# Moving the tail of each batch in a two-layer transformer kernel: transposes, router and feed-forward issued some tenths of a step later

## The reference

```python
qkv = x @ qkv_w + qkv_b                       # 16 heads of 16, a window of 128 keys
local = softmax(mask(q k^T / 4)) @ v
remote = latent_attention(x) @ rout_w + rout_b # 64 pooled tokens per sequence, 4 heads
gate = sigmoid(local @ gl_w + remote @ gr_w)   # one number per row and head
x = layernorm(x + (gate*local + (1-gate)*remote) @ out_w + out_b)

z = (x - mean(x)) * rsqrt(var(x) + eps) * ln_g + ln_b
probs = softmax(batchnorm(mean_over_rows(z)) @ Wr + br); e = argmax(probs)
h = relu(z @ W_down[e] + b_down[e])            # one expert for the whole sequence
x = layernorm(x + (h @ W_up[e] + b_up[e]) * probs[e])
```

## The kernel before

| job | engine, line | what it does |
|---|---|---|
| `gate`, `mix` | DVE, L1450 to L1457 | mixed rows A from local and remote part |
| `turn_a`, `a_in` | PE L1178, ACT L1299 | A transposed, copied to SBUF (two halves) |
| `r`, `r_in` | PE L1102, DVE L1402 | remote part of batch b+1 |
| `out`, `add` | PE L1186, DVE L1461 | output projection, residual sum (two halves) |
| `stats` | DVE, L1345, L1348, L1467, L1468 | means and variances |
| `root` | POOL, L1559 | 1/sqrt of the variances |
| `u_r` | POOL, L1544 | remote part of batch b+1 times a gate weight, 128x1024 |
| `nb` | DVE, L1472, twice | minus mean times 1/sqrt |
| `new` | ACT, L1303 (4) and L1306 (4) | normalised rows z, then the residual x |
| `turned` | ACT, L1270 and three DMA issues L1273 | row maxima of batch b+1 into the stacks |
| `turn_z`, `z_in` | PE L1193, ACT L1311 | z transposed, scaled, column sums |
| `zb`, `rl`, `rl_in` | DVE L1478 to L1480, PE L1199, DVE L1484 | router logits |
| `r_exp`, `choose`, `near` | ACT L1315, DVE L1490, ACT L1321 | expert chosen, its weights copied |
| `h`, `h_in` | PE L1205, ACT L1328 | down projection |
| `up`, `fin` | PE L1214, DVE L1498 | up projection, residual sum (two halves) |
| `stats2`, `root2`, `nb2`, `new2` | DVE L1345 to L1505, POOL L1563, DVE L1508, ACT L1332 | last layer norm |
| `store` | SP, L1018 | x to HBM |

## Time and profile before

### The profile page before, as it was taken

How to read it: one execution, slowest core, us unless ns; L and a number is a source line. 1 busy time by engine, 2 the same in 40 slices (tenths; PEclk the granted TensorE clock), 3 DMA queues, 4 the chain that set the end, 5 groups by cost and what they waited for, 6 DMA issues and landing times. The chain is left out here.

```text
span 1852.8 us, 25416 instructions
## 1 busy us (share of the span) xinstructions
PE 1390.9 (75%) x9117; PEld 880.4 (48%) x9117; DVE 971.0 (52%) x2245; ACT 633.7 (34%) x1201; POOL 292.6 (16%) x278
## 2 busy tenths in 40 slices
PE   4386878887787868714998558988888888888853
PEld 1143445443444445413997325555555555454532
DVE  4254555454545445331776345657474757565622
ACT  0023243333333334302553113344434444434332
POOL 2010001010101000033111311313131313111110
PEclk9678999898999989956999579989898989898966
DMA  3643526353535060085221446426161616060000
GB/s 111 95 80 58 83 56 87 86 74 91 77 87 86 30 89 2 1 267 154 73 70 41 85 77 95 75 41 103 24 103 26 103 31 101 26 89 1 13 12 12
DMA packets 70924, 130.45 MB, mean 70 GB/s; under 512 B 7936, under 2 KB 60816, under 8 KB 67344
## 3 DMA queue, kind: packets, MB, share of 16 engines
q1 hardware_dynamic: 66192, 119.63, 34.2%
q0 software_dynamic: 3072, 8.41, 1.7%
q10 hardware_dynamic: 1536, 0.79, 0.2%
HBM read 84.19 MB, written 43.81 MB: 69 GB/s over the span
## 5 line engine op out<-in xcount | busy, mean ns | idle before, releaser
L467 DVE TENSOR_REDUCE first_maxima<-bank 128x1 f32<-128x512 f32 (+3 forms) x352 | 220.7, 638 | 324.8 <-PE bank L299 323.8
L421 ACT ACTIVATE arena<-pair 128x512 f32<-128x512 f32 x320 | 184.4, 600 | 419.4 <-PE pair L324 418.1
L1416 DVE TENSOR_REDUCE second_maxima<-bank 128x2 f32<-128x512 f32 (+1 forms) x224 | 152.6, 685 | 240.8 <-PE bank L1125 233.2
L1284 ACT ACTIVATE second_probs<-pair 128x512 f32<-128x512 f32 (+1 forms) x256 | 138.2, 543 | 321.0 <-PE pair L1149 279.0
L298 PE MATMUL bank<-first_k_stack,first_q_stack 96*128 96x256 bf16 (+3 forms) x512 | 143.8, 315 | 82.8 <-DMA first_k_stack<-parked 57.6
L323 PE MATMUL pair<-first_q_stack,first_k_stack 99*128 99x512 bf16 (+3 forms) x512 | 138.6, 310 | 10.6 <-DMA first_q_stack<-first_m_turned 8.8
L278 PE MATMUL bank<-first_xT,w_qkv 128*128 128x512 f32 x256 | 133.5, 650 | 11.2 <-DVE first_halves L452 5.6
L1146 PE MATMUL pair<-second_q_stack,second_k_stack 99*128 99x256 bf16 (+1 forms) x512 | 101.2, 283 | 16.8 <-ACT second_probs L1284 13.5
L298 PEld LDWEIGHTS bank<-first_k_stack,first_q_stack 96*128 96x128 bf16 x512 | 51.1, 101 | 124.8 <-DMA first_k_stack<-parked 60.8
L1123 PE MATMUL bank<-second_k_stack,second_q_stack 96*128 96x256 bf16 (+1 forms) x512 | 94.8, 280 | 20.5 <-DMA second_k_stack<-parked 18.7
L342 PE MATMUL pair<-arena,first_values 128*32 128x512 f32 (+3 forms) x1024 | 105.1, 530 | 1.4 <-ACT arena L421 1.4
(11 more groups left out here) (311 smaller groups left out, 2575.7 us busy)
## 6 DMA issues: line engine op xcount, KB each, us to landing
parked<-first_parts SPq DMA_DIRECT2D x32, 384.0 KB, 2.8
first_q_stack<-parked SPq DMA_DIRECT2D x48, 256.0 KB, 8.5
first_k_stack<-parked SPq DMA_DIRECT2D x48, 256.0 KB, 18.9
parked<-second_parts SPq DMA_DIRECT2D x32, 384.0 KB, 2.5
second_q_stack<-parked SPq DMA_DIRECT2D x48, 256.0 KB, 9.0
second_k_stack<-parked SPq DMA_DIRECT2D x48, 256.0 KB, 18.6
sorted_x<-first_zero SPq DMA_DIRECT2D x3, 1670.5 KB, 13.4
expert_xs<-sorted_x SPq DMA_DIRECT2D x39, 128.5 KB, 2.2
```

The source lines that it names most:

```text
L421: act.activation(PT[:, s:s + len(heads), lo:lo + each], ex[n % 3][:, 0:len(heads) * each].rearrange("p (h q) -> p h q", h=len(heads)), ACT ...
L467: dve.tensor_reduce(nm[:, i, qt, heads[0]:heads[0] + len(heads)], mx[n % 2][:, 0:wide].rearrange("p (h k) -> p h k", h=len(heads)), AX.X, ...
L1284: act.activation(PT[:, s:s + len(heads), lo:lo + each], ex[n % 2][:, 0:len(heads) * each].rearrange("p (h q) -> p h q", h=len(heads)), ACT ...
L1416: dve.tensor_reduce(nm[:, i, qt, heads[0]:heads[0] + len(heads)], mx[n % 2][:, :].rearrange("p (h k) -> p h k", h=len(heads)), AX.X, ALU.m ...
```

## The change

Twenty-four kinds of jobs of the tail get other numbers. `turn_a` moves by 0.1 of a step, `out` by 0.08, the first statistics by 0.05 (their later parts by less or a little back), `turn_z` by 0.18, the router's jobs by 0.15 to 0.08, `h` by 0.12, `up` by 0.06 and the last statistics by 0.03. No instruction is added or removed.

```diff
--- before.py
+++ after.py
@@ -900,25 +900,25 @@
         at(t + 1.22, "gate", b)
         at(t + 1.3, "mix", b)
         for c in range(KC):
-            at(t + 1.45 + 0.1 * c, "turn_a", b, c)
-            at(t + 1.55 + 0.1 * c, "a_in", b, c)
-            at(t + 1.76 + 0.1 * c, "out", b, c)
-            at(t + 1.84 + 0.1 * c, "add", b, c)
-            at(t + 2.4 + 0.1 * c, "turn_z", b, c)
-            at(t + 2.48 + 0.1 * c, "z_in", b, c)
-            at(t + 3.42 + 0.1 * c, "up", b, c)
-            at(t + 3.5 + 0.1 * c, "fin", b, c)
+            at(t + 1.55 + 0.1 * c, "turn_a", b, c)
+            at(t + 1.63 + 0.1 * c, "a_in", b, c)
+            at(t + 1.84 + 0.1 * c, "out", b, c)
+            at(t + 1.9 + 0.1 * c, "add", b, c)
+            at(t + 2.58 + 0.1 * c, "turn_z", b, c)
+            at(t + 2.65 + 0.1 * c, "z_in", b, c)
+            at(t + 3.48 + 0.1 * c, "up", b, c)
+            at(t + 3.55 + 0.1 * c, "fin", b, c)
         for n, kind in enumerate(("stats", "root", "nb", "new")):
-            at(t + 2.0 + 0.1 * n, kind, b)
-            at(t + 3.65 + 0.08 * n, kind + "2", b)
-        at(t + 2.7, "zb", b)
-        at(t + 2.8, "rl", b)
-        at(t + 2.88, "rl_in", b)
-        at(t + 2.94, "r_exp", b)
-        at(t + 3.0, "choose", b)
-        at(t + 3.1, "near", b)
-        at(t + 3.2, "h", b)
-        at(t + 3.3, "h_in", b)
+            at(t + 2.05 + 0.08 * n, kind, b)
+            at(t + 3.68 + 0.08 * n, kind + "2", b)
+        at(t + 2.85, "zb", b)
+        at(t + 2.95, "rl", b)
+        at(t + 3.0, "rl_in", b)
+        at(t + 3.05, "r_exp", b)
+        at(t + 3.1, "choose", b)
+        at(t + 3.18, "near", b)
+        at(t + 3.32, "h", b)
+        at(t + 3.38, "h_in", b)
         at(t + 3.97, "store", b)
     return [item[2:] for item in sorted(out)]
```

## The result

| | before | after |
|---|---|---|
| median, us | 1853.03 (20 runs) | 1865.82 (20 runs) |
| lowest to highest, us | 1843.8 to 1861.07 | 1853.1 to 1875.84 |
| the profiled execution, us | 1854.6 | 1854.04 |
| its six periods, `turn_a` of batch 0 to `turn_a` of batch 6, us | 534.04 | 556.78 |

The change made the kernel slower: ratio 1.0081, 95% interval 1.006 to 1.0103, some 13 to 15 us. The median lies at the upper edge of the range given; the direction was forecast wrong.

A forecast was written before the change was run, and what follows sets the result against it. PE was taken to bound layer 1, as ACT and DVE mostly wait for it. The terms, -7.0 - 8.4 + 2.8 + 8.4 = -4.2 us, gave 1850.4 us for the profiled execution, 1849 us median; range 1834 to 1866 us.

The forecast's parts named there:

- clock terms: Low granted clock at PE's pauses: up to 7 x -1.7 us at `turn_a`, 4 x +1.7 at `turn_x`; left out.
- Router and `h`: `up` on PE waits about 0.7 us instead of 0.28, as `turned` precedes `h_in` on ACT: 7 x +0.4 = +2.8 us.
- I cost it at nothing: Jobs from `zb` to `near`, a chain on DVE and ACT beside PE work: no cost.
- `turn_a`: `max` 3 and `exp` 4 fill PE's pause before `turn_a`: 7 x -1.0 = -7.0 us.
- `turn_z`: `nb` freed of `u_r`, z 1.3 us earlier, PE's pause moves to `exp` 5: 7 x -1.2 = -8.4 us.
- a wait of 3 to 4 us: Sign in the profile: PE waits this long for ACT at `exp` 5 (L1146).
- the longest L1423: Sign in the profile: over 1 us right behind `u_r` would mean the hold only changed its victim.
- `stats2` and the store: `stats2` behind `max` 4 on DVE makes `nb2` late; `turn_x` waits about 2.9 us: 4 x +2.1 = +8.4 us.
- (d): Rival: late store lengthens the pause before `turn_x`, low clock follows, DVE's lateness reaches PE; 1872 us; chance 0.08.
- (b): Rival: pauses only move; `turn_a` and `turn_z` gain nothing, losses stay; 1865 us; chance 0.24.
- (c): Rival: clock decides for the change; `turn_a`'s pause too short for low clock, `stats2` not late; 1819 us; chance 0.18.

The follow-up runs named there:

- e1: The kernel before with only the four numbers of `turn_a`, `a_in`, `out` and `add` moved; ratio 0.9987 (0.9952 to 1.0021).
- e4: The changed kernel with `h_in` back ahead of `turned` and its DMA issues on ACT, `h` moved too; ratio to before 0.9948 (0.9912 to 0.9984).
- e10: The kernel before with only the eight lines from `zb` to `h_in` moved (router and `h`); ratio 1.0084 (1.0056 to 1.0111).
- e8: The kernel before with only `u_r` moved, from t-1.9 to t-1.91, ahead of `root` on POOL; ratio 0.9912 (0.9876 to 0.9947).
- e6: The kernel before with only the numbers of `up`, `fin` and the last statistics moved; ratio 1.0134 (1.0095 to 1.0172).
- e2: The kernel before with only the numbers of the first statistics, `turn_z` and `z_in` moved; ratio 0.9968 (0.9932 to 1.0004).
- e9: The kernel before with `u_r` ahead of `root` and the numbers of `turn_a`, `a_in`, `out`, `add` moved; ratio 0.9875 (0.9844 to 0.9907), median 1830.39 us.
- e3: The kernel before with only the numbers from `zb` to `near`, `h`, `h_in`, `up`, `fin` and the last statistics moved; ratio 1.0095 (1.006 to 1.0131).
- e7: The changed kernel with five unused matmuls added on PE in its pause before `up`; ratio to before 1.0016 (0.9992 to 1.0039).

## Why the prediction was wrong

**The step that failed** is the sentence on the sum that the clock terms, "up to 7 x -1.7 at `turn_a`, up to 4 x +1.7 at `turn_x`", "have opposite signs and I leave them out". They didn't cancel, and the largest wasn't among them. The clock was looked for at `turn_a` and at `turn_x`, the places of the long pauses. At `turn_a` alone none was won (e1 has 108.0 us at 0.50, before 104.0). It fell behind `up`, for 10.2 to 17.1 us in five of six batches, at a pause that had been costed at +0.4 us a batch as lost time only.

**Router and `h`, +2.8 us: right place and cause, wrong price.** The order on ACT was read rightly. The pause is 1.36 us instead of 0.28, +1.1 us a batch and not +0.4. The rows ahead of the prediction would have given most of it: `h_in` ended at 1342.38 + 0.67 = 1343.05 and `up` began at 1343.85, 0.80 us later, and the same 0.80 us lie there in after, e4 and e10. With `h_in` ending at 1343.93, as forecast, `up` begins at 1344.73 and has waited 1.16 us; I had let it begin almost at once. The pause alone, +1.1 instead of +0.4 us, is 4.8 us over seven batches. The rest is the clock behind the pause, net 49.6 us more at 0.50 in e10's six periods (153.6 against 104.0) and 24 in a whole execution on average (518 against 494). In place of +2.8 us the term measures +0.84% (0.56 to 1.11%), 15.6 us. For the jobs `zb` to `near`, "I cost it at nothing" isn't contradicted: PE's idle time grew by 4.5 us in e10, less than the 6.5 us of its six longer pauses at `up`.

**`turn_a`, -7.0 us: pauses right, gain not shown.** `turn_a`'s waits fell to some 3 us in total in e1. The ratio, 0.9987, is -2.4 us with an interval from -9 to +4, which holds -7.0 too. Part went to `turn_z`, whose waits grew from 32.6 us to 26.8 + 9.1 = 35.9 us.

**`turn_z`, -8.4 us: mechanism right, but for one wait.** `nb` is free of `u_r`, 0.66 us; the pause moved to `exp` 5 and is 4.1 us, as "a wait of 3 to 4 us" had it; the longest L1423 took 1892 ns against 1884. The size measured alone is 0.9968, -5.9 us (interval -12.6 to +0.7). Left out was `max` 3: with `exp` 3, `max` 3 and `exp` 4 drawn ahead, PE is at the limit of two jobs, and waits 1.10 us for DVE. The two halves of the term have different worth: `u_r` ahead of `root` alone gave 0.9912 (e8), more by its point value than all three lines of `turn_z`, which include it. Whether these give a part of it back isn't settled: the intervals overlap. The bounds of the term hold a slip: without the cost of the second half of `turn_z` it is -1.3 - 0.6 = -1.9 us a batch, and -2.6 is reached only if z also gains 2.0 us.

On `u_r`, the Trainium skill (SBUF — State Buffer, section "SBUF: two separate sides") says that a VectorE instruction with two SBUF inputs waits for the whole of a GpSimd instruction that holds the shared port. The traces agree in both orders: 2.89 us with `u_r` beside `nb`, 0.66 us without, in after, and at most 0.589 us for one instruction in e8.

**`stats2` and the store, +8.4 us: right, and then hidden.** The pause of `turn_x` is 2.7 us where DVE's lateness reaches it (e4, e6), against 2.9 forecast, and `nb2` is 1.8 us later behind `fin`, against 2.1. Taking it out of e4 gave 9 us by the ratios and 16.8 in the periods, against 8.4. Two things were missed. Alone (e6) it cost 1.34%, for the pause brought the low clock in each of four batches (10.2 to 11.2 us at 0.50 between `up` and `turn_a` instead of 2.7 to 3.4), as rival (d) described. In the whole change it isn't what costs: three of four pauses vanish behind PE's slowness.

**The rivals.** (d), "the late store", with 0.08, came nearest in kind: a small pause and behind it a stretch at the low clock. It named 1872 us and `turn_x`; the clock fell at `up` instead. (b), "pauses only move", gave 1865 us, within 1 us of the median, for another reason: it had the gains of the first two terms at nothing, and e1 and e2 together bear out a part of that, but its +2.8 us for `up` is the term that was five times as large. The agreement is a coincidence. (c) forecast that the clock would decide for the change. It does decide, and in e9 for a kernel: -32 us at 0.50.

**What stays open.** Why a pause of 1.36 us before `up` is followed by stretches at 0.50 as long as those around pauses of 2 to 4 us elsewhere, or longer, and in three of 18 cases by none, isn't answered by these runs. Nor is why the time at 0.50 from `turn_a` to `up` fell along with it: in e10 too, where no transpose is moved, it went from 88.7 to 61.5 us. What differs in the rows is what stands around: behind `up` come `up` itself, four matmuls of a projection and many small ones of scores, 48 in 17.10 us at 0.50. That this is the reason wasn't tried. It is open as well by which of its moved pauses e8 got its clock: its five executions lie at a mean clock of 0.872 to 0.879, all of the 18 of before at 0.861 to 0.870, so the clock is no accident of one profile, and at 40 us less at 0.50 it could be the whole of the 16 us.

## What to carry to other kernels

Price a pause of PE by the granted clock behind it and not by its length: here a stretch that began with 1.1 us more of waiting grew by 8.9 us, and filling the wait with useless matmuls won most of the loss against before back. When a job is moved in a list that sets several queues, go through each queue for what it now crosses, DMA issues on ACT included: one 0.67 us copy behind three issues made the difference between a change of twenty-four kinds of jobs that lost 0.8% and one that lost nothing. And look for the small job that holds another: moving `u_r` by 0.01 of a step gave 0.9%, though most of it through the clock.

## What the runs showed of the hardware

- PE stays at the granted clock of 0.50 for long while it is fully busy: 17.10 us of 17.10 in after's batch 1, 27.40 us busy of 27.40 at a mean of 0.69 in e10. At that clock the second `up` takes 1.91 us instead of 1.03.
- A pause of PE before `up` of 1.34 to 1.43 us was followed within 2.2 us by a granted clock of 0.50 in 15 of 18 cases (after, e3, e10), one of 0.15 to 0.46 us in none of 54 (all other kernels).
- Three DMA issues on ACT hold it for 1.80 to 2.31 us in the rows shown, and ACT idles 2.46 us before the copy behind them, more than three times the copy's own 0.68 us.
- From the end of `h_in` on ACT to the start of `up` on PE, which waits for it, 0.80 to 0.83 us pass in before, after, e4, e7 and e10.
- Each part alone was slower than before by 0.84% (e10) and 1.34% (e6), both together by 0.95% (e3), the same within the intervals as the first alone. Here the losses didn't add.
